# One load queue, more staging places and GpSimd's help for the first two units of a two-layer 4096 x 4096 kernel

## The chip, the cores and the metric

The kernel runs on the 8 cores of one Trainium2 chip, each core on its own 2048 rows. A core has TensorE (PE: matmul and transpose), VectorE (DVE), ScalarE (ACT), GpSimd (POOL) and SyncE (SP), which only issues transfers here. ScalarE and GpSimd can issue transfers too; all of a core's transfers run on its 16 DMA engines. The metric is the device time of the slowest core in microseconds (us), lower is better.

## The reference

Input is `x` of shape (2, 8192, 4096), that is 16384 rows of 4096 numbers; both weights are 4096 x 4096. LN is a normalisation of a row: `(v - mean) / sqrt(var + 1e-5)`, without a scale or a bias.

```
block_mask = mask.reshape(128, 32, 128, 32).sum(axis=(1, 3)) > 0       # one bit for each 32 x 32 block
x = x + LN(einsum('bsk,nk->bsn', LN(x), weight1 * block_mask))         # layer 0
x = x + LN(einsum('bsi,oi->bso', LN(x), sign(weight2)) + bias)         # layer 1
```

The change touches only the start of layer 0: the first LN of all rows, the block mask, the masked weights, and the first slab of the product.

## The kernel before, in words

A core's 2048 rows are 16 row tiles of 128. The output columns are cut into 8 slabs of 512. Work goes by units. Unit 0 is slab 0 of row tiles 0 to 7, unit 1 is slab 0 of tiles 8 to 15. From unit 2 to unit 30 a unit is 8 row tiles by one slab: 256 matmuls of 128x512 on TensorE. Those later units read weights block by block (a block is 512 input features by 512 output columns, two pieces of 512 KB) and share each block among 8 tiles that are already normalised and transposed in `HT`.

The first two units are different, since nothing is ready yet. For each row tile k (`x_stats`, L630): its 2 MB of `x` are loaded in two halves; VectorE takes the statistics of 8 pieces (L633), combines them (L636) and works out 1/sqrt in eight small steps on 128x1 columns (`row_scale`, L583 to L596), which are `RS` and `NM` for the tile. ScalarE then writes the normalised tile in bf16 to `HT`, in two halves (L854). TensorE transposes it in 4 groups of 8 (L432, `start_transposes`), each group into a bank of PSUM, and ScalarE copies each group back to `HT` (`evict_transposed`, L799). Then TensorE does the tile's 8 visits, one for each weight block, of 4 matmuls each (`visit`, L442), and ScalarE copies the finished 128x512 result to `YS` (`evict1`, L809), from where GpSimd stores it (`spill`, L920) and VectorE takes its statistics (`y_stats`, L648).

The weights need the mask. A mask piece (512 KB) is reduced on VectorE (`mask_piece`, L604), 4 such pieces give a quarter of a slab's mask through two small products on TensorE (L424, L461) and two small steps on VectorE, and VectorE multiplies the weight pieces by it (`weight_piece`, L628). For row tiles 0 to 3 this goes in four groups j: 4 mask pieces, statistics of tile j, 4 weight pieces (2 blocks). Tile j visits the blocks that exist, and the older tiles visit the two new ones. From tile 4 on all 8 blocks are there. While tiles 4 to 15 pass, the 16 mask pieces and 16 weight pieces of the next slab are loaded and worked as well, for unit 2.

The order of everything is written out by hand in one program for each engine, and every engine runs its program strictly in order. Loads have two queues: SP issues mask and weight pieces, ScalarE issues `x`. Mask pieces share 2 places and weight pieces 3 places of the staging buffer `ST`; a load waits until VectorE has read the piece that was in its place (L316, L318). Tiles of `x` lie, as f32, in the parts of `HT` that no finished tile needs yet (`XHOME`); `XNEED` says how many tiles must be normalised before a tile of `x` can be loaded. In the loop over tiles 4 to 15 TensorE does 4 visits, then all 4 groups of transposes of the next tile, then the other 4 visits:

```
for b in range(8):
    if b == 4 and k < 15:
        start_transposes(k + 1)
    ins = visit(k % 4, k, b, b == 0, b == 7)
```

ScalarE's loop over the tiles is: wait for `xstat`, normalise both halves, issue the next loads of `x`, 4 evictions of transposes, one eviction of a result. GpSimd does nothing before unit 2 but small loads and the stores of results.

## Time and profile before

| | before |
|---|---|
| median of 3 runs (lowest to highest) | 2036.74 us (2034.96 to 2038.03) |
| the profiled execution's own time | 2040.2 us |
| its span (slowest core, core 1) | 2038.7 us |
| spans of the 8 cores | 2021.9 to 2038.7 us |
| TensorE busy | 1857.6 us, 91% |
| VectorE, ScalarE, GpSimd busy | 49%, 25%, 7% |
| mean DMA rate | 231 GB/s |

The span is the time from the first to the last instruction of a core; the profiled execution's time lies 1.5 us above it. The page's 40 slices of the span, 51 us each, show TensorE's busy share in tenths as

```profile
PE   0326789999999999999999999999999999999996
```

so the slices that are not full are the first six and the last.

### The profile page before, as it was taken

The page shows a single profiled execution, that of the slowest core. Times are in us where ns is not written, and L with a number is a line of the kernel's source. Part 1 is how long each engine was busy: PE and PEld are TensorE (multiplying, and loading weights), DVE is VectorE, ACT ScalarE, POOL GpSimd, SP SyncE. Part 2 cuts the span into 40 slices and gives each one's busy share as a digit, 9 for nine tenths or more (in the row PEclk, how much of TensorE's full clock was granted, in tenths as well). Part 3 has the DMA queues.
Part 4 walks back from the last instruction along what each step waited for, and adds up shares of the span by engine and source line. Part 5 has one row for each costly group of instructions (what it writes and reads, how often), then busy time and mean ns, then how long its engine had stood idle before and what let it go on. Part 6 is the DMA issues. An engine that isn't in the chain of part 4 may idle for free.

```text
span 2038.7 us, 26133 instructions; the slowest of 8 cores (2021.9 to 2038.7 us)
## 1 busy us (share of the span) xinstructions
PE 1857.6 (91%) x9483; PEld 875.3 (43%) x9483; DVE 998.2 (49%) x1617; ACT 517.6 (25%) x465; POOL 151.0 (7%) x260
## 2 busy tenths in 40 slices
PE   0326789999999999999999999999999999999996
PEld 0213444444444444444444444444444444444442
DVE  2457676775555444157554344433443034442465
ACT  0315771000000000014345344444431011110032
POOL 0000000000000011011010000000000011000110
PEclk9768999999999999999999999999999999999998
DMA  8645867896779986468669999988892766552384
GB/s 258 192 159 160 274 217 223 264 316 228 241 246 305 293 247 208 145 216 262 229 221 295 287 307 276 301 268 280 268 295 66 229 232 232 191 190 68 110 288 165
DMA packets 121792, 471.54 MB, mean 231 GB/s; under 512 B 13600, under 2 KB 13616, under 8 KB 106304
## 3 DMA queue, kind: packets, MB, share of 16 engines
q1 hardware_dynamic: 80640, 255.89, 41.2%
q0 software_dynamic: 36416, 180.41, 24.8%
q10 hardware_dynamic: 4608, 33.56, 4.9%
q8 instruction: 77, 1.26, 0.2%
q14 instruction: 51, 0.42, 0.1%
HBM read 354.46 MB, written 115.34 MB: 230 GB/s over the span
## 4 chain that ended last, share of the span: by engine, by line
PE 81%; DMA 9%; DVE 4%; ACT 3%; issue 2%; ACTq 0%; DVEq 0%; SPq 0%; POOL 0%; POOLq 0%
PE pb L442 79%; DMA ST<-mask 4%; DMA ST<-w1s 3%; ACT HT L854 2%; PE pb L432 2%; DVE BNX L633 1%; DVE RR L604 1%; DVE RING L628 1%; DMA x1d<-HT 1%; DMA HT<-y1d 1%; ACT HT L799 1%; DMA ST<-x 1%; DMA y1d<-YS 0%; PE pb L424 0%; ACTq L793 0%
## 5 line engine op out<-in xcount | busy, mean ns | idle before, releaser
L442 PE MATMUL pb<-RING,HT 128*128 128x512 bf16 (+1 forms) x8192 | 1778.9, 380 | 6.9 <-ACT HT L799 6.9
L442 PEld LDWEIGHTS pb<-RING,HT 128*128 128x128 bf16 x8192 | 799.4, 98 | 969.4 <-issue 16.1
L717 DVE TENSOR_TENSOR YS<-pb,RR 128x512 bf16<-128x512 f32 x112 | 77.4, 692 | 328.0 <-PE pb L442 328.0
L648 DVE BATCH_NORM_STATS2 BNST<-YS 128x6 f32<-128x512 bf16 x240 | 150.4, 681 | 146.0 <-ACT YS L809 144.8
L809 ACT ACTIVATE YS<-pb 128x512 bf16<-128x512 f32 x128 | 75.2, 597 | 563.7 <-PE pb L442 563.1
L628 DVE TENSOR_TENSOR RING<-ST,ME 128x1024 bf16<-128x1024 f32 x128 | 152.1, 1221 | 116.2 <-PE pb L442 71.2
L604 DVE TENSOR_REDUCE RR<-ST 128x32 f32<-128x1024 int32 x128 | 152.7, 1215 | 105.2 <-DMA ST<-mask 104.2
L815 ACT ACTIVATE RING<-ST 128x1024 fp8e4<-128x1024 f32 x128 | 132.2, 1067 | 189.3 <-DMA ST<-w2s 189.2
L838 ACT ACTIVATE ST<-HT,NM,RS 128x2048 f32<-128x2048 bf16 x32 | 65.7, 2088 | 382.3 <-DVE NM L596 375.8
L432 PE MATMUL pb<-IDN,HT 128*128 128x128 bf16 x1024 | 72.0, 233 | 81.7 <-ACT HT L854 71.8
L799 ACT ACTIVATE HT<-pb 128x1024 bf16<-128x1024 bf16 x128 | 120.3, 1041 | 94.9 <-PE pb L432 91.8
L700 DVE TENSOR_TENSOR HT<-HT,ST 128x1024 bf16<-128x1024 bf16 x64 | 75.6, 1222 | 88.7 <-DMA ST<-x 85.9
L432 PEld LDWEIGHTS pb<-IDN,HT 128*128 128x128 bf16 x1024 | 66.2, 105 | 93.0 <-issue 90.5
L823 ACT ACTIVATE HT<-HT,NM,RS 128x4096 bf16<-128x4096 bf16 x16 | 60.8, 3797 | 148.2 <-DMA x1d<-HT 125.3
L727 DVE TENSOR_TENSOR ST<-ST,HT 128x2048 f32<-128x2048 f32 x32 | 72.2, 2289 | 45.2 <-ACT ST L838 45.2
L920 POOL DMA_DIRECT2D y1d<-YS x32 | 24.4, 763 | 793.9 <-ACT YS L809 793.9
L854 ACT ACTIVATE HT<-HT,NM,RS 128x2048 bf16<-128x2048 f32 x29 | 59.7, 2086 | 80.4 <-DVE NM L596 79.9
L633 DVE BATCH_NORM_STATS2 BNX<-HT 128x6 f32<-128x512 f32 x116 | 70.2, 675 | 19.8 <-DMA HT<-x 14.8
L703 DVE BATCH_NORM_STATS2 BNX<-HT 128x6 f32<-128x512 bf16 x128 | 77.5, 679 | 1.6
L424 PE MATMUL pb<-P,RR 128*32 128x4 f32 x256 | 10.4, 176 | 70.2 <-DVE RR L604 70.2
L920 POOL DMA_DIRECT2D y2d<-YS x28 | 21.5, 768 | 430.9 <-DVE YS L717 428.3
L932 POOL DMA_DIRECT2D ST<-x x64 | 34.3, 538 | 158.4 <-DVE HT L700 156.3
(45 smaller groups left out, 270.4 us busy)
## 6 DMA issues: line engine op xcount, KB each, us to landing
ST<-mask SPq DMA_DIRECT2D x128, 512.0 KB, 9.2
ST<-w1s SPq DMA_DIRECT2D x128, 512.0 KB, 10.1
ST<-w2s SPq DMA_DIRECT2D x128, 512.0 KB, 13.1
ST<-x POOLq DMA_DIRECT2D x64, 512.0 KB, 10.8
out<-ST POOLq DMA_DIRECT2D x32, 1024.0 KB, 6.7
HT<-x ACTq DMA_DIRECT2D x29, 1024.0 KB, 13.0
y1d<-YS POOLq DMA_DIRECT2D x32, 512.0 KB, 4.3
c1d<-RING POOLq DMA_DIRECT2D x32, 512.0 KB, 9.0
```

Of the source, the lines that this page charges most:

```text
L432: ins = t.transpose(PBH[:, b * 1024 + e * 128:b * 1024 + (e + 1) * 128], HT[:, c:c + 128], IDN[:, :])
L442: ins = t.matmul(bank(b), HT[:, c:c + 128], w[:, e * 512:(e + 1) * 512], start=(first and e == 0), stop=(last and e == 3))
L604: v.tensor_reduce(RR[:, (s % 2) * 512 + q * 32:(s % 2) * 512 + q * 32 + 32], stage(("m", g), True).rearrange("p (a b) -> p a b", b=32), AX ...
L628: v.tensor_tensor(dst, src, mk, op=OP.mult).then_inc(sem["wgt"], 1)
L633: ins = v.bn_stats(BNX[:, q * 6:q * 6 + 6], xhalf(k, q // 4)[:, (q % 4) * 512:(q % 4) * 512 + 512])
L648: v.bn_stats(BNST[:, c:c + 6], YS[:, i * 512:(i + 1) * 512]).then_inc(sem["bns"], 1)
L700: v.tensor_tensor(part, part, stage(piece), op=OP.add).then_inc(sem["xp"], 1)
L703: ins = v.bn_stats(BNX[:, q * 6:q * 6 + 6], slot[:, q * 512:(q + 1) * 512])
L717: v.tensor_tensor(YS[:, i * 512:(i + 1) * 512], bank(i), BIA[:, (slab % 2) * 512:(slab % 2) * 512 + 512], op=OP.add).then_inc(sem["ev2"], 1)
L799: a.activation(HT[:, c:c + 1024], PBH[:, b * 1024:(b + 1) * 1024], AF.Identity).then_inc(sem["tev"], 1)
L815: a.activation(ring(n)[:, h * 1024:(h + 1) * 1024], stage(("z", p)), AF.Sign, saturate=False).then_inc(sem["sgn"], 1)
L854: ins = a.activation(HT[:, c:c + 2048], xhalf(k, h), AF.Identity, bias=NM[:, k:k + 1], scale=RS[:, k:k + 1])
```

## The change

It touches units 0 and 1 alone.

- **Places.** Staging places go from 7 to 13: two more lie in `YS`, four in the last four slots of the weight ring `RING`, which are not in use yet. The first 16 mask pieces rotate over 8 places, the first 16 weight pieces over 5, mask pieces 16 to 31 over 5. Each of the first 8 tiles of `x` has a place of its own.
- **Queue.** All loads are issued by SP, in one order: for each group j 4 masks, tile j of `x`, 4 weights; then tile k of `x` and two masks for k from 4 to 11, tiles 12 to 15, and 16 weight pieces. Tiles 8, 9, 14 and 15 wait for the second half of tiles 6, 7, 12 and 13 to be normalised (`xn1`).
- **1/sqrt.** In this phase the small steps leave VectorE for GpSimd (`x_scale`): nine steps on 128x1 columns, each waiting for the one before. VectorE's own `row_scale` (used in later units) has seven steps instead of eight.
- **Normalisation.** ScalarE does the first half of a tile (`norm0`), GpSimd the second (`norm1`), which also waits for the first. From tile 4 on GpSimd's order is `x_scale(k + 1)`, then `norm1(k)`, and ScalarE's `norm0(k + 2)` stands between the evictions of tile k + 1's transposes.
- **TensorE.** In tile k's visits, the first 3 groups of transposes of tile k + 1 come after visit 0 and the fourth after visit 3. The mask products for the next slab come one tile earlier.
- GpSimd's two stores of unit 0 stand behind `norm1(10)` and `norm1(14)`; statistics of results are taken two tiles later on VectorE.

```diff
...
-STAGES = 7
-FEED_RING = (3, 4, 2, 0, 1, 5, 6)
+
+STAGES = 13
+FEED_RING = (1, 2, 3, 4, 0, 5, 6)
 HOME = {}
 BEFORE = {}
...
+    for g in range(16):
+        put(("m", g), ((0, 1, 5, 6), (9, 10, 11, 12))[g // 4 % 2][g % 4])
     for p in range(16):
-        put(("w", p), 2 + p % 3)
+        put(("w", p), (2, 3, 4, 7, 8)[p % 5])
+    for g in range(16, 32):
+        put(("m", g), (g - 16) % 5)
+    last[5] = last[6] = ("xt", 14)
     k = 0
     for u in range(1, 11):
...
-XHOME = [(8, 9), (10, 11), (12, 13), (14, 15), (8, 9), (10, 11), (12, 13), (14, 15),
-         (8, 12), (9, 13), (10, 14), (11, 15), (12, "T"), (13, 15), (14, "T"), (15, "R")]
-XNEED = [0, 0, 0, 0, 1, 2, 3, 4, 7, 7, 8, 8, 9, 12, 13, 14]
-
-SEMS = (["cst", "msk_rd", "wgt", "sgn", "rdy_bt", "rdy_me", "msk_mm", "xstat", "xnorm",
+XHOME = [(k, 8 + k) for k in range(8)] + [(8, 14), (9, 15), (10, "T"), (11, "R"), (12, 14),
+                                          (13, 15), (14, "T"), (15, "R")]
+XNEED = {8: 7, 9: 8, 10: 3, 11: 4, 12: 9, 13: 10, 14: 13, 15: 14}
+XMASK = {10: 12, 11: 16}
+
+SEMS = (["cst", "msk_rd", "wgt", "sgn", "rdy_bt", "rdy_me", "msk_mm", "xaggr", "xstat", "xn0", "xn1",
...
         def stage(piece, ints=False):
             at = HOME[piece][0]
+            if at >= 9:
+                return RINGI[:, (at - 3) * 1024:(at - 2) * 1024]
+            if at >= 7:
+                return YSF[:, (at - 7) * 1024:(at - 6) * 1024]
             return (STI if ints else ST)[:, at * 1024:(at + 1) * 1024]
         def xhalf(k, h):
...
+            def load_x(k):
+                if k in XNEED:
+                    s.wait_ge(sem["xn1"], XNEED[k])
+                if k in XMASK:
+                    s.wait_ge(sem["msk_rd"], XMASK[k])
+                for h in range(2):
+                    s.dma_start(xhalf(k, h), x_d[k * 128:(k + 1) * 128, h * 2048:(h + 1) * 2048]
+                                ).then_inc(sem["ldX%d" % k], 16)
+
             for j in range(4):
-                load_mask(4 * j)
-                load_mask(4 * j + 1)
-                for p in ((0, 1, 2), (3, 4, 5, 6), (7, 8, 9, 10), (11, 12, 13, 14))[j]:
+                for g in range(4 * j, 4 * j + 4):
+                    load_mask(g)
+                load_x(j)
+                for p in range(4 * j, 4 * j + 4):
                     load_w1(p)
-                load_mask(4 * j + 2)
-                load_mask(4 * j + 3)
-            load_w1(15)
-            load_mask(16)
-            load_mask(17)
-            for p in (16, 17, 18):
-                load_w1(p)
-            for g in range(18, 32):
-                load_mask(g)
-            for p in range(19, 32):
+            for k in range(4, 16):
+                load_x(k)
+                if k < 12:
+                    load_mask(2 * k + 8)
+                    load_mask(2 * k + 9)
+            for p in range(16, 32):
...
                 return ins
-            def start_transposes(k):
-                t.wait_ge(sem["xnorm"], k + 1)
-                for g in range(4):
+            def start_transposes(k, groups):
+                for g in groups:
+                    if g == 0:
+                        t.wait_ge(sem["xn0"], k + 1)
+                    if g == 2:
+                        t.wait_ge(sem["xn1"], k + 1)
                     q = 4 * k + g
                     if q >= 3:
...
                 t.wait_ge(sem["tev"], 4 * k + 4)
                 t.wait_ge(sem["ev1"], k - 3)
                 for b in range(8):
+                    if b == 1 and k < 15:
+                        start_transposes(k + 1, range(3))
                     if b == 4 and k < 15:
-                        start_transposes(k + 1)
+                        start_transposes(k + 1, (3,))
                     ins = visit(k % 4, k, b, b == 0, b == 7)
                     if b == 7:
                         ins.then_inc(sem["mm"], 1)
                     elif k == 15:
...
                 v.tensor_tensor(dst, src, mk, op=OP.mult).then_inc(sem["wgt"], 1)
             def x_stats(k):
-                v.wait_ge(sem["ldX%d" % (k % 4)], 32 * (k // 4 + 1))
+
+                v.wait_ge(sem["ldX%d" % k], 32)
+                if k > 0:
+                    v.wait_ge(sem["xaggr"], k)
                 for q in range(8):
                     ins = v.bn_stats(BNX[:, q * 6:q * 6 + 6],
                                      xhalf(k, q // 4)[:, (q % 4) * 512:(q % 4) * 512 + 512])
                 edge(ins)
-                edge(v.bn_aggr(mv(k), BNX[:, :]))
-                row_scale(k).then_inc(sem["xstat"], 1)
+                if k >= 4:
+                    v.wait_ge(sem["xstat"], k - 3)
+                v.bn_aggr(mv(k), BNX[:, :]).then_inc(sem["xaggr"], 1)
...
             mask_bits(7, 0, 4)
+            y_stats(0, 7)
             v.wait_ge(sem["msk_mm"], 10)
             v.tensor_copy(ME[:, 512:1024], bank(7)).then_inc(sem["rdy_me"], 1)
             v.wait_ge(sem["rdy_me"], 5)
-            for q in range(9, 16):
-                if q < 14:
-                    y_stats(1, q - 8)
-            v.wait_ge(sem["xnorm"], 16)
+            for p in range(4):
+                y_stats(1, p)
+            v.wait_ge(sem["xn1"], 16)
...
-                    nxt += 1
+                a.activation(HT[:, k * D:k * D + 2048], xhalf(k, 0), AF.Identity,
+                             bias=NM[:, k:k + 1], scale=RS[:, k:k + 1]).then_inc(sem["xn0"], 1)
+
+            def start_evict(k, g):
+                q = 4 * k + g
+                evict_transposed(k, g, 4 + q % 3, q)
+
+            for k in range(5):
+                norm0(k)
                 for g in range(4):
-                    q = 4 * k + g
-                    evict_transposed(k, g, 4 + q % 3, q)
-                if k == 4:
-                    for p in range(4):
-                        evict1(0, p, p)
-                if k >= 5:
-                    evict1((k - 1) // 8, (k - 1) % 8, (k - 1) % 4)
-            evict1(1, 7, 3)
+                    start_evict(k, g)
+            evict1(0, 0, 0)
+            norm0(5)
+            for k in range(4, 16):
+                if k < 15:
+                    start_evict(k + 1, 0)
+                    start_evict(k + 1, 1)
+                if k < 14:
+                    norm0(k + 2)
+                if k < 15:
+                    start_evict(k + 1, 2)
+                    start_evict(k + 1, 3)
+                evict1((k - 3) // 8, (k - 3) % 8, (k - 3) % 4)
+            for k in range(13, 16):
+                evict1(1, k - 8, k % 4)
...
+            def edge(ins):
+
+                steps[0] += 1
+                ins.then_inc(sem["pool"], 1)
+                g.wait_ge(sem["pool"], steps[0])
+
+            def x_scale(k):
+
+                y = RS[:, k:k + 1]
+                g.wait_ge(sem["xaggr"], k + 1)
+                edge(g.tensor_scalar(VPG[:, :], mv(k)[:, 1:2], EPS, None, OP.add))
+                edge(g.tensor_scalar(y.bitcast(I32), VPG[:, :].bitcast(I32), -0.5, float(RSQ_MAGIC),
+                                     OP.mult, OP.add))
+                for cc in (RSQ_C1, RSQ_C2):
+                    edge(g.tensor_tensor(NTG[:, :], y, y, op=OP.mult))
+                    edge(g.tensor_scalar(NTG[:, :], NTG[:, :], VPG[:, 0:1], cc, OP.mult, OP.subtract))
+                    edge(g.tensor_tensor(y, NTG[:, :], y, op=OP.mult))
+                g.tensor_scalar(NM[:, k:k + 1], mv(k)[:, 0:1], y, -1.0, OP.mult, OP.mult
+                                ).then_inc(sem["xstat"], 1)
+
+            def norm1(k):
+
+                g.wait_ge(sem["xstat"], k + 1)
+                g.wait_ge(sem["xn0"], k + 1)
+                g.tensor_scalar(HT[:, k * D + 2048:(k + 1) * D], xhalf(k, 1), RS[:, k:k + 1],
+                                NM[:, k:k + 1], OP.mult, OP.add).then_inc(sem["xn1"], 1)
+
+            def spill(u, halves=(0, 1)):
                 lay, base, slab = unit(u)
...
                     g.dma_start(out_d[seq * 128:(seq + 1) * 128, h * 2048:(h + 1) * 2048], f_o(k)
                                 ).then_inc(sem["stO%d" % (k % 3)], 16)
-            for u in range(0, 30):
+            for k in range(16):
+                if k < 5:
+                    x_scale(k)
+                if 4 <= k < 15:
+                    x_scale(k + 1)
+                norm1(k)
+                if k == 10:
+                    spill(0, (0,))
+                if k == 14:
+                    spill(0, (1,))
+            for u in range(1, 30):
                 for kind, n in FEED.get(u, []):
...
```

## Rows read from the trace of the kernel before

**Rows 1.** Stretches of 50 us: PE, PEld, DVE, ACT, POOL busy; clock, DMA share, GB/s

```profile
50.00:100.00 50.00, 16.87 (x105) 10.57 (x105) 24.69 (x40) 16.99 (x13) 0.00 (x0) 0.76 0.65 184
100.00:150.00 50.00, 14.13 (x90) 8.27 (x90) 24.27 (x41) 7.85 (x6) 0.00 (x0) 0.67 0.52 173
...
350.00:400.00 50.00, 50.00 (x259) 22.97 (x258) 35.12 (x36) 4.78 (x8) 1.49 (x2) 1.00 0.82 271
```

**Rows 2.** What TensorE waited for up to 340 us: total, times, longest

```profile
PE pb L432 <- ACT HT L854: 71.8, 16, 12.7
PE pb L424 <- DVE RR L604: 69.5, 4, 42.6
```

**Rows 3.** The chain that ended last, in order of time, from 90 us

```profile
93.38 13.86 DMA ST<-mask
...
196.73 4.08 ACT HT L854 x2
```

**Rows 4.** What SP's queue waited for up to 340 us

```profile
SPq L316 <- DVE RR L604: 181.6, 30, 23.2
```

**Rows 5.** TensorE in order of time: the pattern of a tile, and the end of unit 1

```profile
250.54 1.50 PE L432 MATMUL pb<-IDN,HT 128*128 128x128 bf16 x24 [1.77 <-ACT HT L854]
...
313.07 12.26 PE L442 MATMUL pb<-RING,HT 128*128 128x512 bf16 x56
```

**Rows 6.** Stretches of 10 us, columns as in rows 1

```profile
10.00:20.00 10.00, 0.00 (x0) 0.00 (x0) 2.13 (x2) 0.00 (x0) 0.00 (x0) 1.00 0.98 329
20.00:30.00 10.00, 0.00 (x0) 0.00 (x0) 0.00 (x0) 0.00 (x0) 0.00 (x0) 1.00 0.99 297
30.00:40.00 10.00, 0.00 (x0) 0.00 (x0) 1.22 (x1) 0.00 (x0) 0.00 (x0) 1.00 1.01 327
...
300.00:310.00 10.00, 9.07 (x92) 5.38 (x91) 2.72 (x10) 7.29 (x7) 0.00 (x0) 1.00 0.06 24
...
340.00:350.00 10.00, 10.00 (x49) 4.52 (x47) 9.13 (x9) 0.00 (x0) 0.00 (x0) 1.00 1.01 324
```

**Rows 7.** VectorE in order of time: statistics and small steps of tile 0

```profile
43.77 4.83 DVE L633 BATCH_NORM_STATS2 BNX<-HT 128x6 f32<-128x512 f32 x8
...
49.17 0.15 DVE L588 TENSOR_SCALAR VP<-MV 128x1 f32<-128x1 f32 x1
49.43 0.15 DVE L589 TENSOR_SCALAR RS<-VP 128x1 int32<-128x1 int32 x1
...
51.17 0.16 DVE L596 SCALAR_TENSOR_TENSOR NM<-MV,RS 128x1 f32<-128x1 f32 x1
```

**Rows 8.** Groups by line up to 330 us: busy us, mean ns of one

```profile
L799 ACT ACTIVATE HT<-pb 128x1024 bf16<-128x1024 bf16 x64 | 60.4, 1030 | 22.2 <-PE pb L432 19.2 <-issue 3.1
L854 ACT ACTIVATE HT<-HT,NM,RS 128x2048 bf16<-128x2048 f32 x29 | 59.7, 2086 | 80.4 <-DVE NM L596 79.9
...
L604 DVE TENSOR_REDUCE RR<-ST 128x32 f32<-128x1024 int32 x32 | 38.1, 1216 | 80.5 <-DMA ST<-mask 80.4
...
L628 DVE TENSOR_TENSOR RING<-ST,ME 128x1024 bf16<-128x1024 f32 x26 | 30.4, 1219 | 14.8 <-DMA ST<-w1s 14.1 <-DVE ME L658 0.7
```

**Rows 9.** GpSimd in order of time: its only kinds of instruction

```profile
0.53 0.10 POOL L163 MEMSET const-float32-1.0<- 128x1 f32 x1
...
2.78 0.50 POOL L907 DMA_DIRECT2D DK<-dk  x1
...
186.58 0.78 POOL L920 DMA_DIRECT2D y1d<-YS  x1 [182.73 <-ACT YS L809]
```

**Rows 10.** Groups of the whole span (the page): a longer ScalarE step

```profile
L823 ACT ACTIVATE HT<-HT,NM,RS 128x4096 bf16<-128x4096 bf16 x16 | 60.8, 3797 | 148.2 <-DMA x1d<-HT 125.3
```

**Rows 11.** The chain again: from the issue of one weight piece to its landing

```profile
53.04 3.99 DMA ST<-w1s
```

**Rows 12.** VectorE in order of time at the start of unit 2

```profile
317.09 10.29 DVE L628 TENSOR_TENSOR RING<-ST,ME 128x1024 bf16<-128x1024 f32 x9
```

**Rows 13.** TensorE in order of time after an idle stretch: 8 matmuls of 128x512

```profile
62.07 3.57 PE L442 MATMUL pb<-RING,HT 128*128 128x512 bf16 x8 [1.56 <-ACT HT L799]
```

73 lines of the change are left out of this document (29 added, 44 removed).

## The prediction

> **What bounds the kernel now.** I read the table of stretches first. From 350 us on TensorE is busy without a gap and at full clock; between 50 and 150 us it works about 15 us in 50, at a clock of 0.76 and 0.67 [rows 1]. Tile 15, the last of unit 1, starts at 313.1 us (the row holds 56 matmuls, the 32 of tile 15 first) and takes 6.9 us, so unit 2 starts at 320.0 us [rows 5]. All that can be gained lies before that. Then the waits: up to 340 us TensorE waits 71.8 us for a normalised tile and 69.5 us for a reduced mask piece [rows 2]. The chain shows why there are two parts. In the first (tiles 0 to 3, to about 170 us) it is the load of mask pieces, 13.9 us each time [rows 3], and SP's queue shows 181.6 us of waiting for VectorE to free a mask place [rows 4]: a pair of places holds back the whole queue. In the second (tiles 4 to 15) it is the two normalising steps of ScalarE in a row, 4.1 us [rows 3], then transposes, evictions and half a tile of matmuls. The DMA engines are not the bound there: 52% and 65% busy between 50 and 150 us [rows 1], 6% at 300 us [rows 6].
>
> **Part 1: loads in order.** With its engines full the core moves 329, 297 and 327 GB/s, mean 318, and 324 from SP's queue alone at 340 us [rows 6]. A piece of 0.524 MB then takes 1.65 us, a tile of `x` (2.097 MB) 6.6 us, a group j (4 masks, a tile, 4 weights) 19.8 us, a later tile with its 2 masks 9.9 us. A lone load has some 2 us on top: a weight piece lands 3.99 us after its issue, less 1.65 [rows 11]; so a lone tile takes 8.6 us. With the first byte at 3 us, tile 0 is there at 16.2 us, tile 1 at 36.0 us, each next group 19.8 us later. No place holds SP back: a weight piece needs the one five before it read, a mask piece the one eight before.
>
> **Part 2: groups 0 to 3.** Now a circle through the engines is longer than the load. From the statistics of tile j to those of j+1: statistics 5.3 us (43.77 to 49.17 less a short wait [rows 7]), small steps S, ScalarE's half 2.1 [rows 8] with 0.2 for its waits, GpSimd's half N, the last two groups of transposes and their evictions 3.1 (two of 1.03 [rows 8], two of 8 transposes at 0.5 from 24 in 1.50 [rows 5]), the visits of tile j (2, 6, 10, at 0.87 us), and the mask's two products 1.4. For S = 3.6 and N = 3.0 (below) this is 23.9 us from tile 1 to 2 and 27.3 from 2 to 3: statistics of tile 3 start at 36.6 + 23.8 + 27.3 = 87.7 us. Then VectorE: 5.3 + copy 0.3 + 4 weights at 1.25 (1.219 plus a gap [rows 8]) = 98.4; tile 4's statistics 103.7; two masks 2.5; tile 5's end 111.6 us.
>
> **Part 3: GpSimd.** The trace has no arithmetic of GpSimd, only MEMSETs 0.1 us long and the issue of transfers at 0.50 to 0.78 us [rows 9]. Bounds for one of the nine dependent small steps: below, VectorE's simplest step from start to start, 49.43 - 49.17 = 0.26 us [rows 7]; above, GpSimd's longest row, 0.78. I take 0.40, between VectorE's mean step of (51.17 - 49.17)/7 = 0.29 and GpSimd's shortest transfer row of 0.50, since nothing leaves the core here: S = 3.6 us (2.3 to 7.0). For its half tile: below, ScalarE's 2.09 us for the same shape; above, ScalarE's 3.80 us for twice the elements [rows 8, 10]. I take N = 3.0, the middle.
>
> The Trainium skill bears on N: its GPSIMD Engine Reference (Elementwise — side-by-side cycle accounting) gives 1.8 cycles an element as a best case for a tight loop, an estimate of 3.1 us for 2048 elements; by it the sum moves by 1 us. No run here shows it.
>
> **Part 4: what waits for what from tile 4 on.** GpSimd's order is `x_scale(k + 1)`, then `norm1(k)`. So the second half of tile k waits for the statistics, and so for the load, of tile k+1. SP's load of tile 8 waits for `norm1(6)`, which stands behind `x_scale(7)`; the load of tile 9 waits for `norm1(7)`, behind `x_scale(8)`, so behind the landing of tile 8. Tiles 14 and 15 go the same way. Behind the waiting load stands all of SP's queue. These four loads don't overlap with anything; each is a circle of load 8.6 + statistics 5.4 + S + N = 20.6 us. The chain:
> - `x_scale(5)` ends at 111.6 + 3.6 = 115.2, `norm1(4)` at 118.2. TensorE, idle until then, does 2 groups and 5 visits after an idle stretch, at the 1.2 GHz level (8 matmuls in 3.57 us, so 0.43 each [rows 13]): 20 matmuls 8.6 and 0.3 for what the groups add, 127.1. ScalarE evicts and normalises tile 5's half (0.6 + 2.1 -> 129.3), `norm1(5)` 132.3, `x_scale(7)` 135.9, `norm1(6)` 138.9.
> - Tile 8 lands at 147.6, tile 9 20.6 us later at 168.3. Tiles 10, 11 and 12, whose places are free, at 9.9 us each: 197.9. Tile 13, without masks, 204.5.
> - 5.4 + S + N: `norm1(12)` ends at 216.6. Tile 14 lands at 225.2, tile 15 at 245.9, `x_scale(15)` ends at 254.9, `norm1(14)` at 257.9.
> - TensorE stood in tile 13 after its first visit. The other 28 matmuls 6.1, two groups 1.1, 2.6 for the first matmuls after the idle stretch, which go at the lower level: 267.6. Tile 14 with tile 15's transposes 8.9, tile 15 6.9: unit 2 starts at 283.4 us.
>
> Between these circles the engines keep the load's pace: TensorE needs 6.9 + 2.1 = 9.0 us a tile [rows 5], ScalarE 2.1 + 4 x 1.03 + 0.6 = 6.9, VectorE 5.4 + 2.5 + 0.7 = 8.6, GpSimd S + N = 6.6, all under 9.9. VectorE's small steps (2.1 us a tile) are gone from its program at no visible gain, as the load covers them. The interleaved transposes take ScalarE's normalisation off TensorE's path, which was 4.1 us a tile, yet the load comes late in its place. The two stores moved behind `norm1(10)` and `norm1(14)` cost GpSimd 0.8 us each [rows 9], the second before `norm1(15)`, which TensorE needs only 9 us later: nothing. The seven steps in place of eight in later units save 0.3 us beside matmuls: nothing. The mask products one tile earlier wait for tile 15's statistics (251.3), before TensorE asks at 267: nothing.
>
> **Sum.** 320.0 - 283.4 = 36.6 us off the profiled execution's 2040.2 (span 2038.7 and 1.5 around it): 2003.6. The median of the runs is 3.5 us lower than that execution, so the median after is 2000.1 us; I say 2000. After 320 us TensorE has no gap worth a microsecond to lose or to win.
>
> **A rule that speaks against it.** SBUF — State Buffer in the Trainium skill (Who interferes with whom) says that a VectorE instruction with two SBUF inputs and a GpSimd instruction that reads SBUF hold each other off for a whole instruction. Weight pieces are such instructions. No run here shows it yet; what it would do is the third rival.
>
> **Rivals.**
> 1. GpSimd is cheap: S = 2.3, N = 2.1. The chain above holds S 8 times and N 9 times (tiles 1, 2, the stretch from 5 to 7, then 8, 13, 14, 15), so they shed 8 x 1.3 + 9 x 0.9 = 18.5 us: 265, so 1982. For it: dependent steps of VectorE cost 0.29 [rows 7]. Against it: the shortest row of GpSimd with a real effect is 0.50.
> 2. GpSimd is dear, and the change is slower. From S + N = 9.9 us the steady tiles 4 to 13 go at GpSimd's pace as well. At S = 7.0 and N = 3.8: 8 x 3.4 + 9 x 0.8 = 34.4, and some 8 steady tiles at 0.9 over 9.9: 325 us, 5 us later than now. It is slower from S + N of about 10.4 on. At 0.9 us a small step and N = 4.4: S + N = 12.5, 283.4 + 36 + 12.6 + 8 x 2.6 = 353, so 2070. For it: nine round trips a tile where VectorE needed eight, on an engine whose rows reach 0.78 [rows 9].
> 3. In groups 1 and 2 the small steps fall on VectorE's four weight pieces, which hold GpSimd off for up to 4 x 1.22 = 5 us a group [rows 8]: 10 us later, 2010. For it: the steps start just when the weight pieces do. Against it: in the trace GpSimd does no arithmetic, and nothing shows the two engines holding each other.
> 4. The gain is given back in units 2 and 3: there DMA runs at 324 GB/s, share 1.01 [rows 6]. If those loads begin no earlier than now, at most the 20 us of empty DMA around 300 to 320 us come back: 2020. Against it: VectorE starts unit 2's weights at 317.1, 3 us ahead of unit 2 [rows 12]; in the changed kernel it starts after tile 11's result is out (about 274), 9 us ahead, with its places already full.
>
> **Chances.** Forecast 0.43 (its own range 1990 to 2010, a tenth of a microsecond in a small step being worth 7 us), rival 1 0.20, rival 2 0.15, rival 3 0.14, rival 4 0.08. The range that leaves out 2 in 10 runs from 1978 (all of rival 1 but its fastest tail) to 2036 (a third of rival 2 at most within it). What a measurement can tell from no change is about 0.2%, 4 us. Faster by more than that 0.83, within it 0.04, slower 0.13.
>
> **What would show it.** Tile 15 of `x` should land at about 246 us and unit 2 start at about 283. Loads of tiles 8, 9, 14 and 15 should each be issued alone, with some 10 us of little DMA traffic before each. GpSimd's small steps at 0.4 us from start to start and its half tile at 3.0 us; at 0.3 and 2.1 rival 1 holds, at 0.8 rival 2. The mask wait of TensorE (69.5 us) should fall to some 12 us in all. If tiles 8 to 15 are loaded at an even 10 us, my reading of GpSimd's order is wrong, and unit 2 would start 40 us earlier. If weight pieces on VectorE get longer than 1.22 us while GpSimd works, rival 3 is at work.

## The result and the profile after

| | before | after |
|---|---|---|
| median of the runs, us | 2037.38 | 2014.88 (2014.07 to 2015.76) |
| ratio, 95% interval | | 0.9889 (0.9872 to 0.9906) |
| profiled execution, us (its span) | 2040.2 (2038.7) | 2015.76 (2014.2) |
| unit 2 starts, us | 320.0 | 297.9 |
| from there to the end of the span, us | 1718.7 | 1716.3 |

The change makes the kernel 1.1% faster. Forecast were 2000 us, a gain of 36.7 us; it is 22.5. The time lies in the range given, and unit 2 starts 14.5 us later than the 283.4 us of the forecast. In some executions of these kernels the cores of a die show a lower granted clock and take longer: the ratios leave those out, the medians below count them, which moves a median by 0.4 us at most, and of e4_queue_alone, where they were two of four, the other two are given.

TensorE in order of time shows where unit 2 starts. This row holds the last four visits of tile 14 (16 matmuls), the 32 matmuls of tile 15 and then unit 2. At its 52.83/244 = 0.2165 us a matmul, the first 48 take 10.4 us: 287.5 + 10.4 = 297.9 us. The same sum is used for every kernel below. It answers to [rows 5].

```profile
287.49 52.83 PE L461 MATMUL pb<-RING,HT 128*128 128x512 bf16 x244
```

TensorE's waits up to 340 us answer to [rows 2]:

```profile
PE pb L451 <- ACT HT L871: 62.8, 4, 19.8
PE pb L451 <- POOL HT L961: 43.5, 8, 11.9
PE pb L443 <- DVE RR L626: 12.4, 1, 12.4
```

Those of SP's queue answer to [rows 4]:

```profile
SPq L374 <- POOL HT L961: 98.1, 6, 23.5
```

The mask wait fell from 69.5 to 12.4 us, as forecast (12). The wait for a tile that ScalarE normalises is still 62.8 us (71.8 before), but now it is four long waits ahead of tiles 0 to 3 instead of sixteen. New are 43.5 us in which TensorE waits for GpSimd's half, and in SP's queue 98.1 us for the same half: this is the new wait of the forecast.

Stretches of 50 us of the same core (columns as in [rows 1]):

```profile
50.00:100.00 50.00, 23.27 (x121) 12.70 (x122) 23.20 (x28) 11.94 (x10) 14.37 (x19) 0.60 0.89 281
100.00:150.00 50.00, 30.99 (x205) 17.23 (x204) 39.73 (x60) 20.86 (x18) 21.92 (x49) 0.80 0.54 173
```

And of 10 us, which answer to [rows 6]:

```profile
140.00:150.00 10.00, 8.90 (x66) 4.98 (x65) 6.16 (x10) 8.14 (x7) 6.11 (x11) 1.00 0.03 11
...
220.00:230.00 10.00, 10.00 (x72) 5.47 (x71) 4.56 (x9) 6.75 (x8) 7.20 (x16) 1.00 0.00 1
```

Between 50 and 100 us DMA is now 89% busy instead of 65%. Then come holes with next to no transfer. They stand ahead of the loads of tiles 8, 9, 14 and 15. SP's queue shows each of these four issued after a wait of its own (the last two rows are the second halves of tiles 14 and 15; right behind tiles 8 and 9 go two mask pieces each):

```profile
149.70 0.80 SPq L378 DMA_DIRECT2D HT<-x  x2
...
173.56 0.80 SPq L378 DMA_DIRECT2D HT<-x  x2
...
230.49 0.42 SPq L378 DMA_DIRECT2D ST<-x  x1
...
250.78 0.43 SPq L378 DMA_DIRECT2D RING<-x  x1
```

And VectorE's statistics, in order of time, show when each of these tiles has landed (tiles 8, 9, 14, 15):

```profile
162.29 4.85 DVE L658 BATCH_NORM_STATS2 BNX<-HT 128x6 f32<-128x512 f32 x8 [15.97 <-DMA HT<-x]
183.85 4.84 DVE L658 BATCH_NORM_STATS2 BNX<-HT 128x6 f32<-128x512 f32 x8 [13.97 <-DMA HT<-x]
...
239.15 2.48 DVE L658 BATCH_NORM_STATS2 BNX<-HT 128x6 f32<-128x512 f32 x4 [14.06 <-DMA ST<-x]
260.59 2.47 DVE L658 BATCH_NORM_STATS2 BNX<-HT 128x6 f32<-128x512 f32 x4 [15.50 <-DMA RING<-x]
```

GpSimd's arithmetic, which the trace before did not have [rows 9]. Above, the start of the nine steps of tile 0 and its half tile; below, the start of a set of steps in the interleaved part:

```profile
23.49 0.24 POOL L947 TENSOR_SCALAR VPG<-MV 128x1 f32<-128x1 f32 x1 [19.62 <-DVE MV L663]
23.89 1.00 POOL L948 TENSOR_SCALAR RS<-VPG 128x1 int32<-128x1 int32 x1 [0.15 <-POOL VPG L947]
25.03 0.99 POOL L951 TENSOR_TENSOR NTG<-RS 128x1 f32<-128x1 f32 x1
26.20 2.13 POOL L952 TENSOR_SCALAR NTG<-NTG,VPG 128x1 f32<-128x1 f32 x1 [0.18 <-POOL NTG L951]
...
33.90 2.05 POOL L961 TENSOR_SCALAR HT<-HT,RS,NM 128x2048 bf16<-128x2048 f32 x1 [3.65 <-ACT HT L871]
...
127.86 0.22 POOL L947 TENSOR_SCALAR VPG<-MV 128x1 f32<-128x1 f32 x1 [3.13 <-DVE MV L663]
128.24 0.19 POOL L948 TENSOR_SCALAR RS<-VPG 128x1 int32<-128x1 int32 x1 [0.16 <-POOL VPG L947]
128.57 0.20 POOL L951 TENSOR_TENSOR NTG<-RS 128x1 f32<-128x1 f32 x1
128.95 0.30 POOL L952 TENSOR_SCALAR NTG<-NTG,VPG 128x1 f32<-128x1 f32 x1 [0.18 <-POOL NTG L951]
```

What VectorE does beside the held steps is this:

```profile
23.61 3.50 DVE L650 TENSOR_TENSOR RING<-ST,ME 128x1024 bf16<-128x1024 f32 x3 [0.17 <-DVE ME L684]
27.02 1.22 DVE L650 TENSOR_TENSOR RING<-YS,ME 128x1024 bf16<-128x1024 f32 x1
```

The same instruction takes 0.19 us in the lower part and 1.00 us in the upper. Set against VectorE's rows, the upper ones end at 24.89, 26.02 and 28.33 us. The weight pieces begin at 23.61 and then 1.14 us apart, so they change over at about 24.75, 25.89, 27.02 and 28.16: each held step ends 0.13 to 0.17 us behind such a change, and L952, which also takes a number from each partition of a second column (a pointer operand), lets two go by (2.13 us). The weight pieces themselves stay at 1.22 us. So the nine steps take 6.8 us in a group (49.06 to 55.86) and 3.3 us elsewhere (127.86 to 131.15).

### The profile page after: what moved, and what is told of

It reads as the page before. It is cut to its first block, busy times and chain, and to the rows that moved or that the text cites. A ratio compares the mean times of both kernels' runs of the same rounds, so it can differ in the third digit from the quotient of the medians.

```text
span 2014.2 us, 26129 instructions; the slowest of 8 cores (1998.7 to 2014.2 us)
## 1 busy us (share of the span) xinstructions
PE 1866.0 (93%) x9483; PEld 878.1 (44%) x9483; DVE 965.7 (48%) x1441; ACT 484.8 (24%) x449; POOL 231.3 (11%) x420
## 4 chain that ended last, share of the span: by engine, by line
PE 87%; DMA 4%; DVE 4%; POOL 2%; issue 1%; ACT 1%; SPq 0%; DVEq 0%; POOLq 0%; ACTq 0%
PE pb L461 85%; DMA HT<-x 3%; DVE BNX L658 3%; PE pb L451 2%; POOL HT L961 1%; POOL NTG L952 1%; DMA RING<-x 0%; ACT HT L824 0%; DMA ST<-x 0%; PE pb L443 0%; POOL NTG L951 0%; ACT HT L871 0%; POOL RS L948 0%; POOL RS L953 0%; DVE MV L663 0%
## 5 line engine op out<-in xcount | busy, mean ns | idle before, releaser
L650 DVE TENSOR_TENSOR RING<-ST,ME 128x1024 bf16<-128x1024 f32 x122 | 144.8, 1221 | 101.2 <-PE pb L461 73.3
L451 PE MATMUL pb<-IDN,HT 128*128 128x128 bf16 x1024 | 73.8, 233 | 107.9 <-ACT HT L871 62.8
L626 DVE TENSOR_REDUCE RR<-ST 128x32 f32<-128x1024 int32 x120 | 142.3, 1211 | 29.8 <-DMA ST<-mask 28.4
L871 ACT ACTIVATE HT<-HT,NM,RS 128x2048 bf16<-128x2048 f32 x16 | 33.5, 2093 | 88.4 <-POOL NM L954 88.4
## 6 DMA issues: line engine op xcount, KB each, us to landing
ST<-x POOLq DMA_DIRECT2D x64, 512.0 KB, 10.1
HT<-x SPq DMA_DIRECT2D x28, 1024.0 KB, 13.8
```

The source lines that it names most:

```text
L451: ins = t.transpose(PBH[:, b * 1024 + e * 128:b * 1024 + (e + 1) * 128], HT[:, c:c + 128], IDN[:, :])
L626: v.tensor_reduce(RR[:, (s % 2) * 512 + q * 32:(s % 2) * 512 + q * 32 + 32], stage(("m", g), True).rearrange("p (a b) -> p a b", b=32), AX ...
L650: v.tensor_tensor(dst, src, mk, op=OP.mult).then_inc(sem["wgt"], 1)
```

## The experiments

Each kernel was timed in turns with the kernel before. The ratio is to the kernel before on the same chip, with its 95% interval; beside it stands where unit 2 starts on the slowest core of the profiled execution, what is left of its span from there, and the mean start of unit 2 over the 8 cores of that execution.

| kernel | median, us | ratio | unit 2 | rest | mean of 8 cores |
|---|---|---|---|---|---|
| after | 2014.88 | 0.9889 (0.9872 to 0.9906) | 297.9 | 1716.3 | 290.0 |
| e1_norm_first | 1986.12 | 0.9734 (0.9694 to 0.9775) | 262.2 | 1720.9 | 261.2 |
| e2_vector_steps | 1974.14 | 0.9677 (0.9637 to 0.9717) | 251.0 | 1721.7 | 250.3 |
| e3_hold_weights | 2017.15 | 0.9888 (0.9855 to 0.9922) | 295.6 | 1721.0 | 291.6 |
| e4_queue_alone | 1972.95 and 1974.84 | 0.9677 (0.9622 to 0.9732) | 254.4 | 1717.0 | 247.8 |
| e5_scalar_halves | 1992.34 | 0.9776 (0.976 to 0.9791) | 271.5 | 1718.7 | 267.3 |
| e6_double_steps | 2051.29 | 1.0065 (1.0049 to 1.0081) | 332.8 | 1716.2 | 326.3 |
| e7_mixed | 1968.85 | 0.9658 (0.9641 to 0.9676) | 247.1 | 1722.4 | 243.4 |
| e8_mixed_warm | 1966.39 | 0.9652 (0.9637 to 0.9667) | 245.5 | 1718.4 | 242.1 |
| e9_tile8_alone | 2016.13 | 0.9906 (0.9872 to 0.994) | 294.3 | 1720.3 | 289.6 |
| e10_hold_all | 2008.45 | 0.9852 (0.9836 to 0.9869) | 288.8 | 1718.0 | 282.9 |
| e11_reordered | 1969.85 | 0.9674 (0.965 to 0.9699) | 251.5 | 1717.0 | 247.5 |

The rest is 1716 to 1722 us in all twelve: whatever is won or lost before unit 2 is won or lost in the end, and differences below some 6 us between two profiled executions say nothing by themselves. Cores of one execution differ more: in after, unit 2 starts between 283.7 and 297.9 us. The means over the cores follow the medians to 3 us and help to judge a small effect.

### e1_norm_first: is it GpSimd's order that makes the loads serial?

```
                 if k < 5:
                     x_scale(k)
+                norm1(k)
                 if 4 <= k < 15:
                     x_scale(k + 1)
-                norm1(k)
```

> GpSimd does norm1(k) ahead of x_scale(k + 1) instead of behind it; nothing else changes. Theory A (the order on GpSimd ties the load of tiles 9, 14 and 15 to the landing of the tile before): the idle stretches of the DMA engines before tiles 8, 9, 14 and 15 shrink from about 20 to 3 us each, unit 2 starts near 262 us instead of 298, and the time is 2015 - 36 = 1979 us (1970 to 1990). Rival B (the load chain would wait anyway, for places or for VectorE): within 4 us of 2015.

1986.12 us, 28.8 us less than after (36 were expected); the mean start of unit 2 moves by the same 28.8. SP's queue issues tile 9 at 156.8 us, 8 us behind tile 8 and not 24, and the hole in DMA ahead of tile 9 closes. The stretch in e1:

```profile
150.00:200.00 50.00, 43.21 (x310) 24.70 (x308) 34.14 (x52) 29.94 (x28) 19.11 (x48) 0.93 1.00 322
```

TensorE's waits up to 340 us in e1:

```profile
PE pb L461 <- ACT YS L834: 13.8, 4, 6.8
...
PE pb L451 <- POOL HT L961: 1.5, 2, 1.1
```

In after TensorE waits 43.5 us for GpSimd's half, here 1.5; the two lone loads that remain (tiles 8 and 14) show as the 13.8 us behind ScalarE. So the order in GpSimd's program was the cause: shown.

### e2_vector_steps: the nine steps back on VectorE

```
...
-                v.bn_aggr(mv(k), BNX[:, :]).then_inc(sem["xaggr"], 1)
+                edge(v.bn_aggr(mv(k), BNX[:, :]))
+                row_scale(k).then_inc(sem["xstat"], 1)
...
-                if k < 5:
-                    x_scale(k)
-                if 4 <= k < 15:
-                    x_scale(k + 1)
                 norm1(k)
```

> The nine small steps go back to VectorE (seven steps there), so GpSimd only does its half tile, as soon as ScalarE's half is done. Theory A: this takes away both the tie between loads (36 us) and the hold by the weight pieces in groups 0 to 2 (S falls from 6.8 to 2.1 us in each, 14 us), and costs some 0.8 us a tile in tiles 4 to 11, where VectorE becomes the slowest at 10.7 us a tile: 2015 - 36 - 14 + 6 = 1971 us. Rival B (VectorE is too full and the small steps were moved for a reason): 2010 us or more.

1974.14 us, 40.7 less than after. Most of that is e1's gain, since with the steps gone from GpSimd `norm1(k)` has nothing in front of it; against e1 it is 12 us (the mean start of unit 2: 10.9), though the intervals of the two ratios overlap. The prediction had the move of these steps off VectorE as "no visible gain"; it was a loss. On VectorE the steps take 1.9 us. The half tile is now the one that falls on the weight pieces. GpSimd's row of tile 1 in e2:

```profile
51.69 4.44 POOL L958 TENSOR_SCALAR HT<-HT,RS,NM 128x2048 bf16<-128x2048 f32 x1 [17.76 <-ACT HT L868]
```

and three of VectorE's four weight pieces beside it:

```profile
50.88 3.49 DVE L650 TENSOR_TENSOR RING<-ST,ME 128x1024 bf16<-128x1024 f32 x3
```

It ends at 56.13, 1.76 us after the last weight piece (54.37). Alone it takes 2.05 us.

### e3_hold_weights: weight pieces wait for the nine steps

```
+                v.wait_ge(sem["xstat"], j + 1)
                 for p in range(4 * j, 4 * j + 4):
                     weight_piece(p)
```

> In groups 0 to 3 VectorE waits for GpSimd's small steps before it starts the four weight pieces. Theory A (the steps at 1.0, 1.0 and 2.1 us are held off by the weight pieces' second read): all nine steps of a group take 3.3 us instead of 6.8; three groups are shorter by 3.4 us, the weight pieces of group 3 come 3.4 us later: about 2015 - 7 = 2008 us. Rival B (those steps are slow for another reason, as a first use or the state of GpSimd): S stays at 6.8 us, VectorE loses the wait, 2018 to 2025 us.

2017.15 us: the forecast of 9 us was a miss, though the steps did what was expected. GpSimd in e3, third step of tile 0 and half tile of tile 1:

```profile
25.20 0.19 POOL L952 TENSOR_TENSOR NTG<-RS 128x1 f32<-128x1 f32 x1
...
53.75 4.19 POOL L962 TENSOR_SCALAR HT<-HT,RS,NM 128x2048 bf16<-128x2048 f32 x1 [2.37 <-ACT HT L872]
```

0.19 us instead of 0.99, and the nine steps 3.3 us instead of 6.8; but the weight pieces came some 3.5 us later and fell on the half tile, which took 4.19 us instead of 2.05. The hold-off was moved, not removed. The groups still got shorter (the statistics of tile 3 start 81.6 us behind tile 0's, in after 86.6); but the held weights of group 3 put tile 4's statistics 13.5 us behind tile 3's instead of 10.2, and in the end nothing is left. That called for e10.

### e4_queue_alone: the loads alone, all else as before

```
-STAGES = 7
-FEED_RING = (3, 4, 2, 0, 1, 5, 6)
+STAGES = 13
+FEED_RING = (1, 2, 3, 4, 0, 5, 6)
...
+XHOME = [(k, 8 + k) for k in range(8)] + [(8, 14), (9, 15), (10, "T"), (11, "R"), (12, 14),
```

with SP's one queue in order of need; the steps stay on VectorE, both halves on ScalarE, and the transposes are not interleaved. Three small parts of the change are still in it: seven steps for 1/sqrt instead of eight, the mask products one tile earlier, and transposes that can start after the first half of a tile.

> Only the load queue and the places of the change: small steps on VectorE, both halves of a tile on ScalarE, all four groups of transposes after visit 3, results evicted as in the kernel before. Theory A: the loads are the larger part of the gain. Groups 0 to 3 take about 25 us each, tile 4 starts near 115 us, then 12 tiles at the old 11.3 us: unit 2 starts near 258 us, 1975 us, clearly faster than the whole change. Rival B (the split and the interleaving carry the gain, and the loads alone run into ScalarE): 2015 us or more.

1974 us on the mean of the two, a ratio of 0.9677. The load queue and its places, with those small parts, give 3.2%; the whole change gives 1.1%. The three other parts (steps on GpSimd, shared normalisation, interleaving) together cost 2.1%. TensorE in order of time in e4, without interleaving:

```profile
138.20 1.06 PE L451 MATMUL pb<-IDN,HT 128*128 128x128 bf16 x16
140.02 0.61 PE L451 MATMUL pb<-IDN,HT 128*128 128x128 bf16 x8 [0.77 <-ACT HT L873]
...
141.27 7.07 PE L461 MATMUL pb<-RING,HT 128*128 128x512 bf16 x32
```

A tile takes TensorE 10.0 us (138.20 to 148.17), and 8.7 us when interleaved (231.93 to 240.62 in after). VectorE's statistics of tiles 9 and 10 in e4 start 10.1 us apart:

```profile
162.34 4.83 DVE L654 BATCH_NORM_STATS2 BNX<-HT 128x6 f32<-128x512 f32 x8
...
172.43 2.46 DVE L654 BATCH_NORM_STATS2 BNX<-HT 128x6 f32<-128x512 f32 x4
```

No wait for data stands before either, nor before those of tile 11. With the steps back on it, VectorE needs 10.1 us for a tile with its masks and a result's statistics, and sets the pace here, a little above the load's 9.9. So interleaving can win next to nothing on these tiles.

### e5_scalar_halves: steps on GpSimd, both halves on ScalarE

```
+                a.wait_ge(sem["xn0"], k + 1)
+                a.activation(HT[:, k * D + 2048:(k + 1) * D], xhalf(k, 1), AF.Identity,
+                             bias=NM[:, k:k + 1], scale=RS[:, k:k + 1]).then_inc(sem["xn1"], 1)
```

> The small steps stay on GpSimd and the second half of a tile goes back to ScalarE, so GpSimd has nothing that could stand behind x_scale(k + 1). Theory A (the order on GpSimd is the loss, not its small steps): near the kernel with norm1 first, 1986 us, and 1978 to 1992; the small steps of groups 0 to 2 are still held off by the weight pieces (S 6.8 us). Rival B (a wait for S itself is the loss): 2005 us or more.

1992.34 us. No half tile stands behind a statistic of the next tile, and the loads come closer (tile 9 is issued 10.1 us behind tile 8). It is 6 us slower than e1 (the mean start of unit 2 too; the intervals of the ratios overlap), and 18.2 us slower than e2: the held steps are paid in the groups (tile 3's statistics start 87.9 us behind tile 0's, in e2 78.2 us). That is half of it; the other half comes later and was not traced.

### e6_double_steps: nine more small steps for each tile

```
                 edge(g.tensor_scalar(VPG[:, :], mv(k)[:, 1:2], EPS, None, OP.add))
+                for _ in range(9):
+                    edge(g.tensor_scalar(NTG[:, :], VPG[:, :], 1.0, None, OP.mult))
```

> The changed kernel with nine more small steps in each x_scale, writing a scratch column that nobody uses; S grows by 9 x 0.37 = 3.3 us. Theory A (the chain holds S eight times): 8 x 3.3 = 27 us more, 2042 us (2034 to 2048), slower than the kernel before. Rival B (S lies mostly beside loads): under 10 us more, below 2025.

2051.29 us, 36.4 us more than after, at 9 x 0.36 = 3.3 us a tile (133.05 to 136.36). The time lies above the expected 2034 to 2048. The forecast of 27 was eight times 3.3; by the medians and by the mean over the cores (36.3 us) it is eleven times. Counted from the start of tile 0's statistics, the lag over after on the slowest cores grows to 6.8 us at tile 3, 16.9 at tile 8 (three sets of extra steps, where the prediction had two), 19.8 at tile 9 (one), 27.3 at tile 14 (two, where it had one), 29.9 at tile 15 and 33.3 at unit 2 (one each). The 6.8 at tile 3 are three sets as well, one for each period: a set of steps grows there from 6.8 to 9.7 us (53.50 to 63.24), which makes 8.8, and the visits of tiles 0 to 2 happened to take 2.0 us less on this core. The steps stand in series with the loads: shown.

### e7_mixed: each engine where it costs least

Steps on VectorE; ScalarE does both halves of tiles 0 to 4, where weight pieces run; GpSimd does the second half from tile 5 on; interleaved transposes.

```
             for k in range(5):
                 norm0(k)
+                a.wait_ge(sem["xn0"], k + 1)
+                a.activation(HT[:, k * D + 2048:(k + 1) * D], xhalf(k, 1), AF.Identity,
...
-            for k in range(16):
-                if k < 5:
-                    x_scale(k)
-                if 4 <= k < 15:
-                    x_scale(k + 1)
+            for k in range(5, 16):
                 norm1(k)
```

> Small steps on VectorE, both halves of tiles 0 to 4 on ScalarE, GpSimd's half only from tile 5 on, interleaved transposes. Theory A (in groups 0 to 3 every GpSimd instruction that reads is held off by the weight pieces, the half tile as well, 4.2 us in place of 2.05): tile 4 begins as early as with the loads alone (118 us, against 126 with GpSimd's half), then the interleaved tiles at 8.7 us: 1974 - 8 = 1966 us. Rival B (the gain of 8 us is eaten by the waits for tiles 8 and 15): 1972 to 1975.

1968.85 us, near the 1966 expected, and 5 us below e2 and e4, whose intervals overlap with its own (mean start of unit 2: 6.9 us before e2's, 4.4 before e4's).

### e8_mixed_warm: dummy products ahead of the first tiles' transposes

```
+                if j > 0:
+                    for _ in range((0, 100, 100, 100)[j]):
+                        t.matmul(pb[:, 3 * 512:3 * 512 + 128], IDN[:, :], IDN[:, :],
+                                 start=True, stop=True)
                 start_transposes(j, range(4))
```

> As the kernel before it in this call, with 100 matmuls of 128x128 by the identity, whose result is not used, ahead of the transposes of tiles 1, 2 and 3, where TensorE idles 9.3 us. Theory A: transposes and visits of groups 1 to 3 then run at the 2.4 GHz level instead of 1.2 (visits of tile 2: 8.7 instead of 10.8 us; transposes 2 x 1.1 instead of 2 x 1.9 us), 2 to 4 us a group, 8 us in all: 1958 us. Rival B (the path of a group is ScalarE and VectorE and the clock costs nothing): within 2 us of the kernel before it.

1966.39 us, 2.5 less than e7, not the 8 expected. TensorE in order of time in e8, from the dummies of tile 2 on:

```profile
64.92 5.76 PE L488 MATMUL pb<-IDN 128*128 128x128 bf16 x100
74.29 1.42 PE L451 MATMUL pb<-IDN,HT 128*128 128x128 bf16 x16 [3.61 <-ACT HT L872]
76.48 1.87 PE L451 MATMUL pb<-IDN,HT 128*128 128x128 bf16 x16 [0.77 <-ACT HT L882]
80.02 11.27 PE L461 MATMUL pb<-RING,HT 128*128 128x512 bf16 x40 [1.67 <-ACT HT L825]
```

Short stretches of the same; the granted clock is the third number from the right:

```profile
65.00:70.00 5.00, 5.00 (x91) 5.00 (x92) 4.79 (x10) 0.00 (x0) 0.00 (x0) 1.00 1.04 312
80.00:85.00 5.00, 4.98 (x12) 1.74 (x13) 1.40 (x2) 0.00 (x0) 0.00 (x0) 0.50 1.04 384
```

The dummies run at the 2.4 GHz level (clock 1.00), but end 3.6 us before the transposes, whose own stops of 0.8 and 1.7 us follow; the visits start at the 1.2 GHz level all the same (0.50) and take 11.27 us, not 8.7. On two other cores of this execution the same visits, behind a gap of 3.6 and 3.7 us, took 8.79 us, which is the full rate; in e7 they took 10.35 to 10.83 us on every core. So the dummies do not help on every core. Whether filling the gap to its end would help on every core was not tried.

### e9_tile8_alone: why did tile 8 take 12.6 us to land?

```
                 load_x(k)
+                if k in (8,):
+                    s.wait_ge(sem["ldX%d" % k], 32)
```

> The changed kernel, with SP waiting for tile 8 of x to land before it issues masks 24 and 25. Theory A (later transfers of the same queue share the engines with earlier ones, so tile 8 lands 12.6 us after its issue and not 8.6): it lands after 9 us, everything behind it comes 3.6 us earlier: 2011 us. Rival B (a lone tile needs 12.6 us anyway): lands after 12 to 13 us, 2015 us or a little more.

2016.13 us where 2011 were expected: a miss. On the slowest core tile 8, issued at 151.3 us, lands at 160.9, in 9.6 us instead of 12.6. But that does not show that the two mask pieces behind it had taken 3 us. On the 8 cores of after, which run the same program, tile 8 takes 7.5 to 12.6 us (mean 9.4), and here 7.6 to 10.3 (mean 8.7); in e5, with the mask pieces behind it, it takes 9.9 us on the slowest core. The means differ by 0.7 us, far less than the cores among themselves. The mean start of unit 2 moves by 0.4 us. Why one core's load takes 7.5 us and another's 12.6 stays open.

### e10_hold_all: the weights of groups 0 to 2 wait for GpSimd's half

```
                 if j == 3:
                     v.wait_ge(sem["msk_rd"], 16)
+                else:
+                    v.wait_ge(sem["xn1"], j + 1)
```

> The changed kernel, with the weight pieces of groups 0, 1 and 2 waiting until GpSimd's half tile of the group is done, so that no GpSimd instruction meets one. Theory A (the hold is on every GpSimd instruction that reads; holding the weights for the small steps alone only moved it to the half tile): S = 3.3 and N = 2.05 us in these groups, each 3.4 us shorter, 10 us in all: 2005 us. Rival B (VectorE becomes the bound of a group when its weight pieces wait): 2013 us or more.

2008.45 us, 6.4 less than after. GpSimd in e10, a small step of tile 0 and the half tile of tile 1:

```profile
26.06 0.19 POOL L953 TENSOR_TENSOR NTG<-RS 128x1 f32<-128x1 f32 x1
...
56.16 2.04 POOL L963 TENSOR_SCALAR HT<-HT,RS,NM 128x2048 bf16<-128x2048 f32 x1 [2.36 <-ACT HT L873]
```

TensorE in e10: transposes of tile 1, the 24 matmuls of its visits, the 40 of tile 2's:

```profile
56.24 1.86 PE L451 MATMUL pb<-IDN,HT 128*128 128x128 bf16 x16 [10.72 <-ACT HT L873]
...
61.65 5.34 PE L461 MATMUL pb<-RING,HT 128*128 128x512 bf16 x24 [1.63 <-ACT HT L826]
...
85.45 8.79 PE L461 MATMUL pb<-RING,HT 128*128 128x512 bf16 x40 [1.58 <-ACT HT L826]
```

and the same three of TensorE in after:

```profile
58.29 1.87 PE L451 MATMUL pb<-IDN,HT 128*128 128x128 bf16 x16 [14.27 <-ACT HT L871]
...
63.71 8.20 PE L461 MATMUL pb<-RING,HT 128*128 128x512 bf16 x24 [1.33 <-ACT HT L824]
...
92.96 10.70 PE L461 MATMUL pb<-RING,HT 128*128 128x512 bf16 x40 [1.33 <-ACT HT L824]
```

Neither steps nor half are held now. The periods of the statistics, 29.25 and 31.74 us in after, are 23.70 and 26.43, against 23.9 and 27.3 forecast. Of the gain from tile 1 to 2, 3.5 us are GpSimd's steps and 2.9 the visits, at 0.22 instead of 0.34 us a matmul; 0.8 is lost again, as the mask's reduction now comes late. The shorter visits are not this edit's doing, though TensorE waits only 10.7 us ahead of them and not 14.3. In e1 the same visits follow the same long wait and are as short:

```profile
57.70 1.86 PE L451 MATMUL pb<-IDN,HT 128*128 128x128 bf16 x16 [14.26 <-ACT HT L871]
...
63.11 5.34 PE L461 MATMUL pb<-RING,HT 128*128 128x512 bf16 x24 [1.33 <-ACT HT L824]
```

The granted clock is 1.00 there (63 to 69 us), and 0.50 in after from 63 to 67. On the 8 cores of after these visits take 5.34 to 8.26 us behind equal waits. The means over the cores leave most of this out: tile 3's statistics come 7.2 us earlier behind tile 0's, and unit 2 7.1 us earlier. That is the worth of keeping GpSimd clear in groups 0 to 2, less than three times 3.5, since the held weights come later.

### e11_reordered: tiles 10 and 11 loaded ahead of 8 and 9

```
-            for k in range(4, 16):
+            for k, g in ((4, 16), (5, 18), (6, 20), (7, 22), (10, None), (11, None), (8, 24), (9, 26),
+                         (12, 28), (13, 30), (14, None), (15, None)):
```

> The warm mixed kernel, with tiles 10 and 11 of x, whose places are free early, loaded ahead of tiles 8 and 9. Theory A (the DMA engines idle while the queue's head waits for tile 6, and the two tiles fill that time): unit 2 starts 8 us earlier, 1958 us (1955 to 1962). Rival B (TensorE is bound by its own 8.7 us a tile from there on, or tile 8 comes later behind the two): 1964 us or more.

1969.85 us, 3.5 more than e8, on which it is built: a miss. VectorE in e11 at tile 8:

```profile
151.43 4.85 DVE L661 BATCH_NORM_STATS2 BNX<-HT 128x6 f32<-128x512 f32 x8 [7.90 <-DMA HT<-x]
```

and TensorE behind it:

```profile
163.37 1.86 PE L462 MATMUL pb<-RING,HT 128*128 128x512 bf16 x4 [8.64 <-ACT YS L836]
```

Tile 8 is issued at 136.2 us as in e8 (135.7), but tiles 10 and 11 are still on their way; it lands 15.2 us later, in e8 11.7. The ranges over the cores do not touch: 13.6 to 15.8 us here, 8.8 to 11.7 in e8. They filled the hole in DMA (share 1.04 between 130 and 135 us, in e8 0.13) and pushed the one tile that TensorE needs next.

## Why the prediction was right in kind and wrong in size

The mechanism holds point by point: one queue frees the masks, the second half stands behind the next tile's statistics, and four loads run alone. The size does not: 2014.88 us lies within 1978 to 2036, but outside the 1990 to 2010 that the forecast called its own range, and above rival 3's 2010. At each mark, forecast and trace of the slowest core (us):

| | forecast | trace | late by |
|---|---|---|---|
| statistics of tile 3 start | 87.7 | 104.6 | 16.9 |
| `norm1(6)` ends | 138.9 | 149.6 | 10.7 |
| tile 8 landed | 147.6 | 162.3 | 14.7 |
| tile 9 landed | 168.3 | 183.8 | 15.5 |
| `norm1(12)` ends | 216.6 | 230.0 | 13.4 |
| tile 15 landed | 245.9 | 260.6 | 14.7 |
| unit 2 starts | 283.4 | 297.9 | 14.5 |

From tile 8 on the trace stays 13.4 to 15.5 us late. The whole error is made before, in the groups of Part 2 above all:

- **S in the groups, 3.6 us forecast and 6.8 measured.** The estimate of a free step was good (3.3 us for nine, 0.37 each, against 0.40). The price was another one: rival 3, given 0.14, is true. Its "against", that nothing in the trace before showed the two engines holding each other, was empty, since GpSimd did no arithmetic there; absence from such a trace should not have lowered the chance. e3 and e10 show the cause, and e10 prices it: 6.4 us off the median, 7.1 off the mean start of unit 2 (rival 3: 10). The sign that the prediction named for it was wrong: weight pieces stayed at 1.22 us; they were under way first, and GpSimd is the one that waits. The Trainium skill, SBUF — State Buffer (Who interferes with whom), has the mechanism: a VectorE instruction with two SBUF inputs contends with a GpSimd instruction that reads SBUF. The trace agrees: 1.00, 0.99 and 2.13 us for steps of 0.19, 0.20 and 0.30.
- **Visits of tiles 0, 1 and 2, 1.7, 5.2 and 8.7 us forecast, 3.28, 8.20 and 10.70 measured.** They start at the 1.2 GHz level on this core. The prediction used that level behind tile 5 and forgot it here, though [rows 13] is such a row. Which core is hit is chance as far as the runs show: tile 1's visits take 5.34 us on two other cores.
- **Tile 0 to tile 1, 20.4 us forecast, 25.6 measured.** The prediction's 36.6 for tile 1's statistics is 16.2 plus its own circle with two visits, which comes to 20.4 (the load alone would give 36.0); its count of eight S leaves this one out. The 5.2 us too many are 3.2 for the held steps, 1.5 for the visits and 1.3 for a term that the sum did not have, a table that ScalarE loads before its first step (row below), less 0.9 for the half tile. The late terms of the three periods make 5.2 + 5.35 + 4.4, and tile 0 landed 1.8 us later than 16.2: together the 16.8 at tile 3.
- **The half tile, 3.0 us forecast and 2.05 measured** (rival 1's 2.1). Three of them and the free S gave back 2.9 of the 6.2 us that lie between tile 3 and the end of `norm1(6)`. The Trainium skill, GPSIMD Engine Reference (Elementwise — side-by-side cycle accounting), gives 1.8 cycles an element as the best case, an estimate of 3.1 us; here the measurement decides, at a third less.
- **The visits behind `norm1(4)`, 8.9 us forecast and 6.0 measured** (133.20 to 139.21). The prediction had TensorE idle before them and the visits at the 1.2 GHz level; it was at the visits of tiles 0 to 3, waited 1.1 us and ran at 0.22 us a matmul. That gave back another 2.9 us: the lower level was forecast where it did not come and left out where it did.
- **A lone load, 8.6 us forecast.** On the slowest core tile 8 took 12.6, tile 9 10.3, tiles 14 and 15 9.0 and 10.2; over the 8 cores tile 8 took 7.5 to 12.6, mean 9.4. So the estimate was near, and the slowest core is slow in part by its loads. From tile 8 to 9 this and the cheap half tile nearly cancel: a circle is 21.6 us against 20.6. That the lateness stays even from tile 8 on is luck in that measure.

The table load, between tile 0's small steps and ScalarE's half:

```profile
30.33 1.28 ACT L871 ACT_TABLE_LOAD   x1 [30.33 <-POOL NM L954]
```

Two slips in the working: 127.1 + 0.6 + 2.1 is 129.8 and not 129.3, and "No place holds SP back" is not so. Up to 340 us SP's queue waits 110.2 us for weight pieces to be read, 28.5 at the longest. It cost little: of tiles 1 to 7 only tile 7 comes late for VectorE, by 1.4 us.

The count of eight sets of steps in the chain was low; e6 finds eleven where they are doubled. Rival 2 is false by S + N = 5.35 us. Rival 4 is false: VectorE begins unit 2's weights at 290.0 us, 8 us ahead, and the rest of the span is no longer than before.

What the prediction did not ask is which part earns the gain. It found the serial loads, called them the new bound, and left it there. By e4 the loads alone bring 3.2%, and the three other parts take two thirds of it back: the order on GpSimd (e1: 28.8 us) and the steps held by the weight pieces (e10: 6.4 us), while interleaving and the shared half tile have little to give, because TensorE does not pace these tiles: the load or, with the steps on it, VectorE does. The best version measured is e8 with 1966.39 us, 0.9652 (0.9637 to 0.9667) of before; the dummies in it are worth 2.5 us at most, so e7 is the one to keep.

Open: what decides whether visits behind a wait start at the lower level. After 14.26 us of waiting tile 1's visits took 8.20 us in after and 5.34 in e1, and in e7, after only 9.3 us, those of tiles 1 and 2 took 0.30 and 0.27 us a matmul. The length of the wait does not decide. Open too is why cores of one execution differ by 14 us in the start of unit 2 and by 5 us in one load.
